# Rotary embedding of three chunks moved to GpSimd, padding rows loaded by DMA, q and k columns sorted by parity

## The reference

```python
q = layernorm(q, q_gamma, q_beta)
k = layernorm(k, k_gamma, k_beta)
q = q * cos + rotate_half(q) * sin      # rotate_half: (-odd elements, even elements)
k = k * cos + rotate_half(k) * sin
scores = where(tril, scale * q @ k.T, -inf); out = softmax(scores) @ v; out @ Wo.T + bo
```

## Time and profile before

| | us |
|---|---|
| median of 3 executions | 516.39 (515.0 to 517.4) |
| the profiled execution, its own time | 514.6 |
| its span in the profile | 512.9 |
| TensorE busy / VectorE / ScalarE / GpSimd | 395.9 / 380.5 / 271.9 / 190.2 |
| mean granted TensorE clock, share of full | 0.876 |

### The profile page before, as it was taken

The page is one execution under the profiler, slowest core; times in us unless marked ns, Lnnn a source line. Parts: engine busy times, 40 slices in busy tenths (PEclk is TensorE's granted clock), DMA queues, the critical chain, the costliest instruction groups (busy, mean ns, idle before and its releaser), DMA issues.

```text
span 512.9 us, 8026 instructions
## 1 busy us (share of the span) xinstructions
PE 395.9 (77%) x2663; PEld 201.8 (39%) x2663; DVE 380.5 (74%) x806; ACT 271.9 (53%) x483; POOL 190.2 (37%) x270
## 2 busy tenths in 40 slices
PE   1812078858779687879999995998887999989696
PEld 0410042213443433433332452554353335467484
DVE  7689999899988579974574887498999751167454
ACT  1420032735369310566769773539553987875464
POOL 6127421463201470352325312724221413664353
PEclk9955567779879786989999998799998999997979
DMA  5704013000220700000002205200044000000620
GB/s 135 142 0 123 0 42 84 2 3 3 66 63 4 164 1 0 3 0 1 22 3 53 73 2 128 41 2 1 2 83 85 23 1 1 1 1 1 129 59 20
DMA packets 29866, 20.10 MB, mean 39 GB/s; under 512 B 8890, under 2 KB 29659, under 8 KB 29819
## 3 DMA queue, kind: packets, MB, share of 16 engines
q1 hardware_dynamic: 29154, 18.94, 16.5%
q0 software_dynamic: 144, 0.39, 0.3%
q10 hardware_dynamic: 528, 0.26, 0.2%
HBM read 11.99 MB, written 1.18 MB: 26 GB/s over the span
## 4 chain that ended last, share of the span: by engine, by line
DVE 40%; PE 38%; ACT 8%; DMA 7%; issue 6%; POOL 1%; SPq 0%; POOLq 0%; ACTq 0%
PE psum L763 9%; DVE mx_diag L1155 8%; DVE mx_full L1155 8%; PE psum L812 6%; PE psum L745 5%; PE psum L720 5%; ACT probs L873 3%; DMA comb_b<-combine_scratch 3%; DVE roped L1118 3%; PE psum L686 3%; DVE roped L1132 2%; PE psum L800 2%; PE psum L714 2%; PE psum L801 2%; DVE seed L1061 2%
## 5 line engine op out<-in xcount | busy, mean ns | idle before, releaser
L873 ACT ACTIVATE probs<-psum 128x1024 f32<-128x1024 f32 x144 | 142.1, 1029 | 58.0 <-PE psum L745 53.7
L1155 DVE TENSOR_REDUCE mx_diag<-psum 128x4 f32<-128x512 f32 (+2 forms) x96 | 96.7, 1038 | 33.6 <-PE psum L720 33.2
L1034 POOL TENSOR_SCALAR_AFFINE_SELECT probs<-probs 128x256 f32<-128x256 f32 (+1 forms) x112 | 50.4, 466 | 97.9 <-ACT probs L873 96.7
L1045 POOL TENSOR_TENSOR mh<-mh,mv 128x256 f32<-128x256 f32 x72 | 56.4, 794 | 79.0 <-DVE mh L1242 68.7
L763 PE MATMUL psum<-probs,v_ones 128*16 128x512 f32 (+3 forms) x768 | 80.5, 509 | 1.9 <-POOL probs L1034 1.5
L1155 DVE TENSOR_REDUCE mx_full<-psum 128x2 f32<-128x1024 f32 x64 | 74.8, 1215 | 8.0 <-PE psum L720 7.7
L720 PE MATMUL psum<-k_st,q_st 62*128 62x512 bf16 (+3 forms) x384 | 64.2, 365 | 16.5 <-DVE mx_full L1155 14.6
L812 PE MATMUL psum<-w,mh 128*128 128x128 f32 x288 | 54.7, 328 | 18.3 <-POOL mh L1045 16.2
L745 PE MATMUL psum<-q_st,k_st 64*128 64x512 bf16 (+3 forms) x384 | 57.2, 343 | 10.2 <-ACT probs L873 4.0
L910 ACT ACTIVATE mu<-psum,b1h 128x256 f32<-128x256 f32 x72 | 34.1, 473 | 57.3 <-PE psum L801 35.7
L561 POOL TENSOR_TENSOR mv<-mv,comb_b 128x256 f32<-128x256 f32 x48 | 35.7, 744 | 77.0 <-ACT mv L912 64.0
(11 more groups left out here) (138 smaller groups left out, 448.5 us busy)
## 6 DMA issues: line engine op xcount, KB each, us to landing
comb_b<-combine_scratch SPq DMA_DIRECT2D x16, 512.0 KB, 8.2
q_st<-parts SPq DMA_DIRECT2D x24, 128.0 KB, 2.4
k_st<-parts SPq DMA_DIRECT2D x21, 128.0 KB, 2.5
w<-in_We SPq DMA_DIRECT2D x3, 512.0 KB
out<-xs SPq DMA_DIRECT2D x4, 256.0 KB, 2.3
xs<-in_x SPq DMA_DIRECT2D x3, 256.0 KB, 5.2
q_st<-maxT SPq DMA_DIRECT2D x32, 4.0 KB
k_st<-parts POOLq DMA_DIRECT2D x3, 128.0 KB, 3.7
```

The source lines that it names most:

```text
L873: act.activation(probs[:, n % P_RING, :, :], wpair("scores", (s, i)), ACT.Exp, scale=SCALE).then_inc(exp_done, 1)
L1034: last = pool.affine_select(out=v, in_=v, compare_op=ALU.is_ge, fill=0.0, base=0, pattern=[[0, v.shape[1]], [1, P]], channel_multiplier=-1)
L1045: pool.tensor_tensor(mh[:, at % MOE_RING, :], mh[:, at % MOE_RING, :], mv[:, at % MOE_RING, :], ALU.mult).then_inc(h_ready, 1)
L1155: dve.tensor_reduce(dst[:, qt, :, pairs[0]:pairs[0] + nm], w, AX.X, ALU.max).then_inc(max_free, 1)
```

## The change

- The rope becomes one helper, `rope_of`, of six instructions over both queries and keys: scale by `hrstd` (in place in `qk`), cosine into `sq`, two sine instructions into `roped`, add the shift, add both. VectorE runs it for chunk 0, GpSimd for chunks 1 to 3. `headscale` and `rope_sum` are gone.
- The columns of the projection are sorted by parity of the head, so the arrays are `[tile, q/k, parity, element, head pair]`. ScalarE writes the squares with heads and elements exchanged.
- The tables are built per half: the first on VectorE, the second on GpSimd (`tables_pool`).
- The memsets of `q_st` and `k_st` are gone. Four DMAs from a new input `c_pad` write rows 6 and 7 of every eight; they are issued on the SP queue after the load of chunk 1 and before those of chunks 2 and 3. The DMAs of ones are gone.
- `v_ones` has 9 columns a head; GpSimd sets only the ninth, for both batch elements at the start.
- All six stack DMAs of the first keys are issued by ScalarE.
- The bf16 copies of identity and mask, and the halved bias, are stages of their own (`consts`, `halved`).
- The planner's assumed durations are new, it knows that `gated`, `weight_dve` and `rope` take longer beside some work of GpSimd, and the stages changed as above. The windows and `PV_LAG` keep their values, so the order is a new one made with the old windows.

The core of the diff:

```diff
-VC = 16
+VC = HD + 1
 LENGTHS = {
...
-    "pool": {"ones": 1.9, "xbo": 1.3, "rope_pool": 4.9, "qT_low": 1.2, "kT_low": 1.2, "mask": .5,
-             "weight": .75, "stack_pool": 3.2, "moe_h": .75},
-    "sp": {"stack": 3.9, "mrow": 1.3, "cstore": .6, "cload": 1.2, "store": .6},
+    "pool": {"ones": .3, "xbo": 1.25, "rope_pool": 11.0, "tables_pool": 2.5, "qT_low": 1.12, "kT_low": 1.12, "mask": .55,
+             "weight": .72, "moe_h": .72},
+    "sp": {"stack": 2.0, "mrow": 1.3, "cstore": .6, "cload": 1.3, "store": .6},
...
-DMA_DONE = {"stack": 6.1, "stack_pool": 8.5, "mrow": 2.6, "cstore": 2.3, "cload": 4.7,
+DMA_DONE = {"stack": 4.4, "stack_act": 4.4, "mrow": 2.6, "cstore": 2.3, "cload": 9.0,
             "store": 3.0}
+LOCKING = {"tables_pool": .2, "rope_pool": 1.1, "qT_low": 1.1, "kT_low": 1.1, "weight": .7, "moe_h": .7, "xbo": 1.2}
+LOCKED = ("gated", "weight_dve", "rope")
...
+            if engine == "pool":
+                held = kind, now + took
+            if kind in LOCKED and held[0] in LOCKING and held[1] > now:
+                took += min(held[1] - now, LOCKING[held[0]])
...
+ROPE_OF = ("rope", "rope_pool", "rope_pool", "rope_pool")
...
+        def rope_of(engine, x, chained):
...
+            plain = sq[:, :, :, :, :, :].rearrange("p t w r a b -> p (t w r a) b")
+            chained(engine.tensor_tensor(
+                heads(qk), heads(qk), hrstd[:, :].rearrange("p (n m) -> p n m", m=H // 2).unsqueeze(2).broadcast_to(
+                    [P, TPC * 4, HD, H // 2]), ALU.mult))
+            engine.tensor_tensor(plain, flat(qk), table(g_cos), ALU.mult)
+            sin = g_sin[:, c, :, :, :, :].rearrange("p t w r d -> p (t w r) d")
+            for j in range(2):
+                last = engine.tensor_tensor(heads(roped)[:, :, 4 * j:4 * j + 4, :], heads(qk)[:, :, 1 - j::2, :],
+                                            sin[:, :, 4 * j:4 * j + 4].unsqueeze(3).broadcast_to([P, TPC * 4, 4, H // 2]),
+                                            ALU.mult)
+            chained(last)
+            chained(engine.tensor_tensor(plain, plain, table(g_add), ALU.add))
+            return engine.tensor_tensor(flat(roped), flat(roped), plain, ALU.add)
...
             for i in range(1, NX):
                 sp.dma_start(xs[:, i, :, :], x_v[i]).then_inc(ld_x[i], 16)
-            sp.dma_start(causal[:, :], c_causal).then_inc(ld_moe, 16)
+                if i == 1:
+                    for t in range(len(TERMS_Q), HD):
+                        sp.dma_start(k_st[t::HD, :, :, :].rearrange("p b m q -> p (b m q)").bitcast(F32),
+                                     c_pad).then_inc(ld_pad, 16)
+                        sp.dma_start(q_st[t::HD, :, :, :].rearrange("p x m q -> p (x m q)").bitcast(F32),
+                                     c_pad[:, 0:H // 2 * CH]).then_inc(ld_pad, 16)
...
+            def rope_turned(x):
+                pool.wait_ge(rstd_ready, x)
+                pool.wait_ge(work_full, turned("kT", x - 1))
+                rope_of(pool, x, link).then_inc(roped_ready, 1)
...
                 if kind == "ones":
-                    if arg == 0:
-                        pool.memset(q_st[:, :, :, :].rearrange("p x m q -> p (x m q)").bitcast(F32), 0.0).then_inc(q_set, 1)
-                    pool.memset(k_st[:, arg, :, :].rearrange("p m q -> p (m q)").bitcast(F32), 0.0).then_inc(k_set, 1)
-                    pool.memset(v_ones[:, arg, :, :, :], 1.0).then_inc(v_set, 1)
+                    pool.memset(v_ones[:, arg, :, :, HD:VC], 1.0).then_inc(v_set, 1)
...
+                elif kind == "stack_act":
+                    stack(act, *arg, stacked[0])
```

More of the change, by code:

```diff
@@ L99 @@
 LENGTHS = {
[L100 to L105, removed]
@@ L117, with bank_options @@
+READY_AT = {"weights": 6.0, "norm": 4.5}
 PE_TICK, PE_BUSY = 3.413, 1.3
 SIGNAL = 0.12
+def bank_options(kind):
+    if kind in PAIR_BANKS:
+        return PAIR_BANKS[kind]
+    return tuple((q,) for q in SINGLE_BANKS if q != Y_BANK or kind not in ("moe", "cT"))
 def plan():
@@ L140, in stacked_last @@
     def stacked_last(x, which):
-        return ("stack", (x, which, 1)) if (x, which) != (0, 1) else ("stack_pool", 0)
+        return ("stack" if (x, which) != (0, 1) else "stack_act", (x, which, 1))
     def old(kind, arg, ok):
@@ L150, in plan @@
     add("tables", 0, -20, ("norm", 0))
+    add("tables_pool", 0, -15, ("tables", 0))
+    add("consts", 0, -20, ("tables", 0))
+    add("halved", 0, -2, ("norm", 2))
     add("ones", 0, -40)
-    add("ones", 1, -11, ("kT_low", 0))
+    add("ones", 1, -39)
     def window(lo, hi, what):
@@ L198, in plan @@
         key = lo + u * (hi - lo) / count
-        add("max", (a, u), key, *[stacked_last(y, w) for y in range(x - x % 2, x + 1) for w in range(2)],
+        add("max", (a, u), key, ("consts", 0), *[stacked_last(y, w) for y in range(x - x % 2, x + 1) for w in range(2)],
             old("max", units[n - 1], n))
@@ L283, in plan @@
     for stage, m in missing.items():
-        ready_at[stage] = {"weights": 8.0, "norm": 5.0}.get(stage[0], 0.0)
+        ready_at[stage] = READY_AT.get(stage[0], 0.0)
         if not m:
@@ L294, in banks_for @@
     def banks_for(kind, arg, now):
-        if kind in PAIR_BANKS:
-            return next((pair for pair in PAIR_BANKS[kind] if all(is_free(q, now) for q in pair)), None)
         if kind in FILLS_READ:
-            return next(((q,) for q in SINGLE_BANKS if is_free(q, now) and (q != Y_BANK or kind not in ("moe", "cT"))), None)
+            return next((banks for banks in bank_options(kind) if all(is_free(q, now) for q in banks)), None)
         if kind == "moe_y" and arg[1] == 0 and not is_free(Y_BANK, now):
@@ L302, in banks_for @@
         return ()
-    now, work = 0.0, {}
+    now, work, held = 0.0, {}, (None, 0.0)
     while len(order) < len(needs):
@@ L570, in stack @@
                 engine.wait_ge(work_full, turned(*LAST_SCORES[NG * (x - 1) - 1]))
-            if which == 0 and c == 0 and not lower:
-                engine.wait_ge(q_set, 1)
-                engine.wait_ge(k_set, b + 1)
-                for par in range(2):
-                    engine.dma_start(k_st[ROWS * par + KM:ROWS * (par + 1), b, :, :].rearrange("p m q -> p (m q)").bitcast(F32),
-                                     c_ones.partition_broadcast(2)).then_inc(ld_ones, 16)
             for part in (1, 2) if lower else (0,):
@@ L833, in _ @@
                     pe.wait_ge(roped_ready, arg + 1)
-                    turn(kind, arg, lambda t, w=which: roped[:, w, t, :, :, :].rearrange("p r d m -> p (r d m)"))
+                    turn(kind, arg, lambda t, w=which: roped[:, t, w, :, :, :].rearrange("p r d m -> p (r d m)"))
                 elif kind == "max":
@@ L1056, in link, with rsqrt @@
                 dve.wait_ge(chain, links[0])
-            def rsqrt(out, v, n):
+            def rsqrt(out, v, n, ready=None):
                 y, half, sq_v = seed[:, 0:n].bitcast(F32), nr[:, 0, 0:n], nr[:, 1, 0:n]
@@ L1067, in rsqrt @@
                                                     op0=ALU.add, op1=ALU.mult)
-                    link(last)
+                    if step < 2 or ready is None:
+                        link(last)
+                if ready is not None:
+                    last.then_inc(ready, 1)
             def norm(kind, x):
```

208 lines of the change are left out of this document (88 added, 120 removed).

## The result

| | before | after |
|---|---|---|
| median, us | 515.69 | 531.91 |
| the single executions, us | 515.0, 516.39, 517.4, 514.77 | 525.81, 532.48, 532.58, 531.34 |
| the profiled execution / its span | 514.6 / 512.9 | 525.81 / 524.1 |
| mean granted clock | 0.876 | 0.839 |

The changed kernel is slower: the ratio is 1.0284, with a 95% interval of 1.0202 to 1.0366. The forecast was 495 us and faster. The execution with a profile is the shortest of the changed kernel's four, so the profiles explain 525.8 - 514.6 = 11.2 us of the 16.2 between the medians.

What follows compares the result with a forecast made beforehand. VectorE was taken to bound the start; from 87 to 446 us no engine is full, TensorE busiest at 86%. Start 19, later ropes 6, less GpSimd's queue 3 and order 2: 514.6 - 19 - 6 + 3 + 2 = 494.6, forecast 495, range 474 to 517.

Steps and rivals of the forecast that it cites:

- The new order: New stage list under unchanged urgencies: a loss of 2 us taken, bounded at 13 us either way.
- Rival E: Old urgencies put ropes or maxima of chunks 2 and 3 where TensorE has nothing else: slower, 519 to 524; chance 0.10.
- Start: Work up to the first scores and chunk 0's maxima: 14.6 to 24 us earlier, 19 taken.
- rope of chunk 0: On VectorE before the first scores: 6.4 us instead of 8.9, saving 2.5; `roped` ready at 29.2.
- Rope of chunk 1 on GpSimd: Moved from VectorE: takes 12.2 us, ends at 52.4, so chunk 1's keys come 14.6 us earlier.
- Memsets: GpSimd's memsets stall VectorE; removal saves 3.55 us in norm 0 and 5.72 at chunk 1's head deviation.
- Ropes of chunks 2 and 3: Moved to GpSimd: VectorE loses 17.9 us of work, 6 us gain taken; GpSimd's longer queue costs 3.
- Rival A: The port lock shared by VectorE and GpSimd eats the relief from moving three ropes: 503 us; chance 0.12.
- Padding: DMAs of 1.5 MB ahead of chunks 2 and 3 on SP hold transfers 7 us, covered: 0 taken.
- D: The padding DMAs are late and delay the first maxima by 8 us: 503 us; chance 0.05.
- B: TensorE's little room hides the gain, half of the 25 us goes: 504 us; chance 0.14.
- C: All of the gain carries, 24 us at the start and up to 18 later: 473 to 484 us; chance 0.13.

Runs made afterwards that it cites:

- e1: The changed kernel's instructions in the stage order and PSUM banks of the kernel before: 499.1 us, ratio 0.9703 to the kernel before.
- e4: The changed kernel in its own order, with the ropes of chunks 2 and 3 on VectorE: 525.7 us, ratio 1.0233 to the kernel before.
- e8: The kernel before, planned with the changed kernel's assumed durations, instructions and windows as before: 538.4 us, ratio 1.0457.
- e10: The changed kernel, planned with the old assumed durations, no lock rule and old windows: 525.4 us, ratio 1.0186 to the kernel before.
- e7: e1 with GpSimd's old memsets back, on an extra tile that nothing reads: 506.3 us, ratio 0.9842 to the kernel before.
- e6: e1 with the ropes of chunks 2 and 3 on VectorE: 501.3 us, ratio 0.9744 to the kernel before.
- e12: e2 with the ropes of chunks 2 and 3 on VectorE: 467.0 us, ratio 0.9061 to the kernel before.
- e2: The changed kernel with its windows and PV_LAG searched anew for the earliest planner's own end: 461.2 us, ratio 0.8969 to the kernel before.
- e5: The changed kernel with only the window of chunk 1's experts moved later and widened: 511.1 us, ratio 0.9949 to the kernel before.
- e3: The kernel before with its windows searched anew in the same way as e2: 518.7 us, ratio 1.0064.
- e11: The changed kernel with a planner knowing slower small VectorE stages beside GpSimd ropes and maxima landing behind router weights, windows searched again: 468.5 us, ratio 0.9083.

## Why the prediction was wrong

**The step that failed** is "The new order": "the urgencies are unchanged while the preparation windows now hold fewer stages ... I bound it by a quarter of that either way (13) and take a loss of 2." Measured by e1 against the changed kernel it is 32.8 us, two and a half times the bound (26.0 us between the two profiled executions, twice the bound). The bound was drawn from TensorE's 52 idle microseconds, as if an order could only shift idle time that is there. It can make new idle time: between 87 and 446 us 359 - 294.1 = 64.9 us, in spite of a start that was 14 us ahead. 22.0 us are lost between unit 10 and unit 12, where the list puts 13 expert units instead of 8, and the norm of chunk 2 ahead of the maxima of unit 12.

**Rival E was right** in its cause, and near in its price: "with the old urgencies the ropes or maxima of chunks 2 and 3 are put where TensorE has nothing else". The maxima of units 11 and 12 do come late, but what stands ahead of them are the norm of chunk 2, router weights and experts of chunk 1, which E didn't name; the ropes play no part there (e4). 26 to 31 us had been named as the cost, and 32.8 came (26.0 by the profiles). Its sign, TensorE idle for over 20 us more in the middle, didn't come: it is 64.9 us instead of 52.0, and part of the loss is a slower clock (0.85 instead of 0.91 from 87 to 446 us), which makes TensorE's busy time longer. What was wrong was its chance of 0.10. "GpSimd is two thirds idle" was the argument against it, and it has no bearing: here it wasn't load that decided, but which stage of a strict list stands before which. e8 and e10 show that the risk was there for other edits of the planner's inputs too.

**The size of the operations** was near. Without the term for the order the sum was 492.6, 22.0 us below the profiled execution; e1 is 15.2 below its neighbour. Its parts:

*Start, 19 taken.* e1 gets its first scores at 76.90 instead of 87.19, 10.3 us earlier, and unit 5 is 14 us earlier. In the changed kernel's own list they come at 72.70. The forecast asked for 68 and called itself wrong beyond 75, which e1 passes and the changed kernel's own list doesn't: by that sign alone the forecast would have stood. The reasons are in the timeline of the changed kernel:

```profile
5.61 0.17 DVE L1091 TENSOR_SCALAR seed<-rstd 128x4 int32<-128x4 int32 x1
...
12.85 0.87 DVE L1105 BATCH_NORM_STATS2 stats<-xs 128x6 f32<-128x128 f32 x4 [3.95 <-DMA xs<-in_x]
16.75 1.65 ACT L969 ACTIVATE xn<-xs,shift,rstd 128x128 f32<-128x128 f32 x4 [3.24 <-DVE shift L1122]
...
26.08 1.23 DVE L581 TENSOR_TENSOR qk<-qk,hrstd 128x1024 f32<-128x1024 f32 x1
...
31.06 1.23 DVE L592 TENSOR_TENSOR roped<-roped,sq 128x1024 f32<-128x1024 f32 x1
...
41.24 1.21 DVE L1127 TENSOR_REDUCE ssum<-sq 128x128 f32<-128x1024 f32 x1
43.97 0.64 PE L752 MATMUL psum<-causal_bf,ident_bf 128*128 128x256 bf16 x2
```

The stalls of the earlier trace rows are gone, 0.17 each as forecast. But most of the 3.55 us is waited away at once: VectorE stands 3.95 us at chunk 1's load, and ScalarE 3.24 us behind it, since the list puts chunk 1's norm ahead of a read of chunk 0's projection. The rope of chunk 0 takes 32.29 - 26.08 = 6.2 us (6.4 forecast), and ends at 32.3 instead of 29.2. The head sums of chunk 1 begin at 41.24, as late as in the earlier trace rows, because the norm of chunk 2 was put ahead. The forecast saved time on a chain and didn't ask what waits for a load next.

*Rope of chunk 1 on GpSimd*, 12.2 us in the forecast:

```profile
47.19 2.35 POOL L581 TENSOR_TENSOR qk<-qk,hrstd 128x1024 f32<-128x1024 f32 x1 [2.83 <-DVE hrstd L1096]
49.62 1.96 POOL L584 TENSOR_TENSOR sq<-qk,g_cos 128x1024 f32<-128x1024 f32 x1
51.54 2.09 POOL L587 TENSOR_TENSOR roped<-qk,g_sin 128x512 f32<-128x512 f32 x2
53.70 1.99 POOL L591 TENSOR_TENSOR sq<-sq,g_add 128x1024 f32<-128x1024 f32 x1
55.77 2.34 POOL L592 TENSOR_TENSOR roped<-roped,sq 128x1024 f32<-128x1024 f32 x1
```

55.77 + 2.34 - 47.19 = 10.9 us. The forecast's reserve, that wide broadcasts cost more than its line and 2 us of the gain go, didn't come true: the two instructions with a table on 1024 elements took 1.96 and 1.99 us instead of 2.41, the other two 2.35. Its end, 58.1, is 8.9 us earlier than before and not 14.6.

*Memsets, 9.3 us of stalls* (3.55 + 5.72): e7 gives 7.2 us of time for them. It doesn't come evenly. In e7 the stalls at the start last 4.0 us, and the head sums of chunk 1 begin only 1.5 us later than in e1 (40.16 and 38.64), as the load of chunk 1 hides the rest; those at the head deviation last 3.7 us and all of it is on the path. First scores come 6.1 us later (83.01 and 76.90).

*Ropes of chunks 2 and 3, 6 - 3 = 3 us*: e6 less e1 is 2.1, not clear of the noise. Near, but the reason was another. Forecast was VectorE busy at "some 340 us"; it was 362.3. These two ropes take VectorE about 13 us in e4 and e6, yet moving them to GpSimd changes its busy time by +2.9 us (e4 to after), -2.8 (e6 to e1) and -2.2 (e12 to e2). So GpSimd's instructions cost VectorE 10 to 16 us elsewhere. Rival A's mechanism is right, its time isn't: of the ropes of chunks 2 and 3 a gain of 5.8 us is left in e2's order, and 2.1 in e1's. VectorE's total falls by less than 3 us in both, so it doesn't give the time; what does was not traced.

*Padding*: the four loads are issued by 10.4 us and land 8.5 and 9.2 us after their issue (medians of `k_st` and `q_st`). The first maxima come at 43.97 and don't wait for them. 0 was right, D wrong.

**Rivals B and C.** B fell with e1: first scores are 10.3 us earlier than before, unit 5 is read 14.6, unit 10 14.7 and the end of the span comes 14.8 us earlier. Nothing of the start's gain is lost behind it. e2 shows besides that TensorE can be kept at 121.6 of 129 us. C's 473 was passed by e2, but with windows that the change doesn't have.

**What stays open.** Shown is that the order makes the loss: the same operations with another list (e1), with one other window (e5). Shown by the traces is where it is made, between unit 10 and unit 12, and what stands in the list there. Not separated is how the 22 us divide. That the old windows suited only the old inputs of the planner is shown for two other inputs (e8, e10). Why just these lists come out bad is not settled, and the planner's own end doesn't say it: it differs by 7.5 us between the two kernels where the chip shows 16.2 (and 32.8 for the order). It did rank the big steps of the changed kernel: 476.7, 457.8, 435.2 became 531.9, 511.1, 461.2. It failed on two others: e3 has a lower end than the kernel before (464.1 against 469.2) and is 0.6% slower, e11 a lower one than e2 under the same planner (441.6 against 448.8) and is 7.4 us slower.

## What to carry to other kernels

Where a list, written out or planned, fixes each engine's order, treat operations and order as two changes: measure the new operations in the old list and then search the list again, before you judge either. Here the operations were worth 15 us in the old order, the list made with the old windows cost 33 and new ones brought 38 more, so that a kernel that looked 3% slower was 10% faster. Compare two lists between the same milestones of the work, as the reads of the units are here: the hole that catches the eye in a window need not be where the time went. And count of the work that is moved to GpSimd what VectorE's total does, not only what leaves VectorE.

## What the runs showed of the hardware

**Small VectorE instructions stand behind GpSimd's.** The norm of chunk 3 falls beside the rope of chunk 2 on GpSimd (81.42 to 92.3). The changed kernel, VectorE's timeline:

```profile
82.40 0.86 DVE L1105 BATCH_NORM_STATS2 stats<-xs 128x6 f32<-128x128 f32 x4
...
83.91 1.94 DVE L1091 TENSOR_SCALAR seed<-rstd 128x4 int32<-128x4 int32 x1
...
88.11 1.81 DVE L1096 SCALAR_TENSOR_TENSOR seed<-nr,seed 128x4 f32<-128x4 f32 x1
...
90.16 2.19 DVE L1095 TENSOR_TENSOR nr<-nr,rstd 128x4 f32<-128x4 f32 x1
...
93.81 0.32 DVE L1122 SCALAR_TENSOR_TENSOR shift<-mean_var,rstd 128x4 f32<-128x4 f32 x1
```

and e4, where VectorE does that rope itself, first:

```profile
81.33 1.21 DVE L582 TENSOR_TENSOR qk<-qk,hrstd 128x1024 f32<-128x1024 f32 x1
...
86.94 1.53 DVE L593 TENSOR_TENSOR roped<-roped,sq 128x1024 f32<-128x1024 f32 x1
88.39 0.86 DVE L1106 BATCH_NORM_STATS2 stats<-xs 128x6 f32<-128x128 f32 x4
...
92.08 0.16 DVE L1123 SCALAR_TENSOR_TENSOR shift<-mean_var,rstd 128x4 f32<-128x4 f32 x1
```

The norm takes 11.7 us beside the rope and 3.9 without it. Rope and norm one after the other on VectorE are done at 92.2 us, side by side on two engines at 94.1: for this pair GpSimd's help is worth less than nothing. An instruction of 0.16 to 0.2 us on four elements lasts up to 2.19, about the length of one GpSimd instruction. By the Trainium skill (SBUF — State Buffer, the section on two separate sides) whoever is first keeps the shared pair of ports for its whole instruction and the other blocks; the trace agrees. What a GpSimd instruction cost here went by its own length and not by the size of VectorE's.

**A small transfer behind large ones.** SP's queue in the changed kernel, and TensorE's first scores after it:

```profile
299.61 3.57 SPq L680 DMA_DIRECT2D comb_b<-combine_scratch  x4
303.23 1.37 SPq L667 DMA_DIRECT2D q_st<-maxT  x2
...
312.53 0.61 PE L782 MATMUL psum<-q_st,k_st 64*128 64x512 bf16 x2 [6.68 <-DMA q_st<-maxT]
```

Four loads of 512 KB stand ahead of two transfers of 4 KB with maxima, the second of which lands 8.45 us after its issue, and TensorE waits for it for 6.68 us. In e1 the same four loads stand ahead and the scores come no sooner behind them (maxima issued at 299.65, scores at 308.72), but TensorE has expert work until then.

**TensorE's clock follows the order.** The granted clock from 296 to 425 us is 0.79 in the changed kernel and 0.95 in e1 with the same instructions. TensorE's busy time over the whole span is 405.2 us in the one and 396.7 in the other. Where TensorE waits between maxima for each reduction it was granted 0.50 to 0.64, so part of an order's price is paid in slower matmuls.
